# Two bursts of scatters moved on GpSimd's queue, and the second norm's application moved on ScalarE's, in a cross-attention and mixture-of-experts kernel

## The chip, the cores and the metric

The kernel runs on one core of a Trainium2 chip. The metric is the device time of one execution in microseconds (us), lower is better. The engines are named as in the profile: PE (TensorE, matmuls), PEld (its weight loads), DVE (VectorE), ACT (ScalarE), POOL (GpSimd) and SP (SyncE, which only issues DMAs here).

## What is computed

x has 4 x 2048 tokens of 512 values, the context 4 x 154. The reference is, cut to what matters:

```python
x = x + xattn(layernorm(x), ctx)          # 16 heads of 32, scores over 154 context rows, softmax, output projection with bias
x = x + ffn(layernorm(x))                 # 8 experts, 512 to 512, the best 2 of each token
# in ffn:
router_logits = einsum('bsd,ed->bse', x, W_router) + b_router
topk_w, topk_idx = top_k(softmax(router_logits), 2)
out = einsum('bseo,bse->bso', einsum('bsd,eod->bseo', x, W_experts) + b_experts, sparse_weights)
```

## The kernel before

**Two phases.** The first phase runs over 16 blocks of 512 tokens (each of 4 tiles of 128 tokens). For a block it computes the first norm, the attention, the sum x1 with the residual, the second norm and the router, and then writes every normalized token twice to a table in HBM (`dispatched`), sorted by expert, with a scatter: one indirect DMA on POOL's queue for each tile of 128 tokens and each of the two choices. The second phase takes 135 tiles of 128 rows of that table one after the other, multiplies each with its expert's weights and adds the result to the output in HBM, again with an indirect DMA on POOL.

**Slots.** The first phase is software-pipelined by hand. Each engine has a function `pe_slot`, `act_slot`, `dve_slot`, `pool_slot`, `sp_slot` that writes out one slot: the steps of several blocks in a fixed order. All engines work through their slots in order and wait for one another by semaphores alone. One slot takes about 50 us in the profile, and a loop repeats them; the first and last slots are written out. In what follows a slot is named by the block b whose scores and exponentials it computes. In that slot the blocks b+1 to b+3 are in their first norm and query projection, block b-1 is in its output projection, and block b-2 is applied its second norm and scattered.

**The steps that the change and the prediction touch**, on POOL in the order of before:
- `pool_PL` (line 1172): the low half of the probabilities P, 128x1024, of parts 0, 2, 3, 5, 7, 8 of a block (parts 1, 4, 6, 9 are DVE's, line 1091). PE's `pe_PV` waits for them.
- `pool_NC` (lines 597 to 615): a chain of eight tiny operations that turns the variances into scale and shift. With n = 0 it is the first norm's of block b+3, with n = 1 the second norm's of block b-1. It waits for `act_norm` (ACT line 582).
- `pool_BX(j)` (line 1248): adds the output bias to the residual of tile j of block b-1. DVE's `dve_Oe(j)` (line 987) waits for it: it adds the output projection, which PE has left in a PSUM bank, and so also frees that bank.
- `pool_RQ` (lines 1192, 1195): prepares the router's logits; DVE's `dve_RB` (line 1012) waits for it. `pool_RP` and `pool_RW` (lines 1206 to 1239): masks, weights and rows of the router for block b-2.
- `pool_SC` and `pool_SD` (line 1252): the two bursts, four scatters each, of block b-2. Both wait for the second norm's result, `act_NY` (ACT line 620).

On PE, `pe_MT` (line 756) turns the row maxima of block b+1 for ACT's `act_MTe` (line 933), and `pe_LB` (lines 851 to 854), right behind it, computes the second part of the router's logits in 36 small matmuls. `pe_LB` may only begin when `dve_Oe(3)` has emptied its bank; behind it stands the seventh query step, `pe_Q` (line 708), which waits for `act_MTe`. From slot 13 on the first norm's chain is no longer there, and in slot 15 PE has neither queries nor maxima left to compute.

In slot 14 DVE also computes a table that assigns tiles to experts (`table_sums`, `table_experts`, `table_rows`, lines 1126 to 1161): some 25 operations on 8 values, which lie between its other steps.

Of the kernel before, what the change touches and what calls it, by code (L numbers as in the profile page):

```python
# [19 lines left out]
NB = N // TB  # L20
# [90 lines left out]
def build(nc, x, ctxT, wqT, bq, wkT, bk, wvT, bv, woT, bo, weT, be, wrT, br, wo, boc, out):  # L111
# [15 lines left out]
    def hold(e):  # L127

        e.sem_inc(tick[id(e)], 1)
# [266 lines left out]
    def act_split(e, n):  # L396

        name, dst, scale = parts_of[n]
        e.wait_ge(L[name], 16)
        src = w_sb[name] if name in w_sb else wr32[:, :, :]  # L400
        e.activation(dst[:, 0, :, :], src, ACT.Copy, scale=scale).then_inc(p_hi, 1)
# [174 lines left out]
    def act_norm(e, n, b):  # L576
        e.wait_ge(nvar[n], b.at(NJ, NJ))
        if b.past(1):
            e.wait_ge(nco[n], b.at(NCO))
        e.activation(nrm[n][:, 1, :], aggr[n][:, :, 1], ACT.Ln, bias=epst[:, 0:1]).then_inc(nln[n], 1)  # L580
        e.wait_ge(nln[n], b.at(1, 1))
        e.activation(nrm[n][:, 2, :], nrm[n][:, 1, :], ACT.Exp, scale=-0.5).then_inc(nrs[n], 1)
# [35 lines left out]
    def act_apply(e, n, b, j, src, dst):  # L618
        e.wait_ge(nco[n], b.at(NCO, NCO))
        e.activation(dst[:, j, 0:D], src[:, j, :], ACT.Identity, scale=nrm[n][:, 5, j:j + 1],  # L620
                     bias=nrm[n][:, 6, j:j + 1]).then_inc(nap[n], 1)
# [6 lines left out]
    def act_NY(e, b, j):  # L628
        if j == 0:
            for k in range(TOPK):  # L630
                if b.past(2):
                    e.wait_ge(scat[b.par][k], b.half(64))
        act_apply(e, 1, b, j, xR[b.par], xn2[b.par])
# [223 lines left out]
    def act_XTh(e, b, i):  # L857
        e.wait_ge(t1p, b.at(4, i + 1))
        if i == 0 and b.past(1):
            e.wait_ge(qp, b.at(4))  # L860
            e.wait_ge(lap, b.at(1))
        e.activation(xnT[0][:, i, :], W[:, BANK[f"XT{i}"], :], ACT.Copy).then_inc(t1h, 1)

    def act_Qh(e, b, G):
        if b.first and G == 0:
            e.wait_ge(p_bk, 2)
        e.wait_ge(qp, b.at(4, G + 1))
        if G == 0 and b.past(1):
            e.wait_ge(restack[1 - b.par], (b + -1).half(192, 192))
        e.activation(qs[0][:, G, :], W[:, BANK[f"Q{3 * G}"], :], ACT.Identity, bias=bqs[:, G:G + 1]).then_inc(qhe, 1)  # L870
        if b.first and G == 3:
            act_split(e, 2)

            e.wait_ge(qle, 4)
            restack_heads(e, b, (2, 3))

    def act_ATh(e, b, i):
        e.wait_ge(atp, b.at(4, i + 1))
        if i == 0 and b.past(1):
            e.wait_ge(op_, b.at(4))  # L880
            e.wait_ge(lbp, b.at(1))
        e.activation(aT[0][:, i, :], W[:, BANK[f"AT{i}"], :], ACT.Copy).then_inc(ath, 1)
# [32 lines left out]
    def exps(n):  # L915

        h = BANK[f"ST{n}"] - 2
        return P32[PLP.index(n) % R32][:, :, :] if n in PLP else S[:, 2 * h:2 * h + 2, :]

    def act_PH(e, b, n):  # L920
        e.wait_ge(exd, b.at(10, n + 1))

        done = (2 * n - 9) // 5 if n >= 5 else (2 * n + 11) // 5 - 4
        if n > 4 or b.past(1):
            e.wait_ge(pvt, b.at(8, 2 * done + 2))
        r = 2 * (n % 5)
        e.activation(Pst[0][:, r:r + 2, :], exps(n), ACT.Copy).then_inc(phd, 1)  # L927
# [241 lines left out]
    def pool_PL(e, b, n):  # L1169
        e.wait_ge(phd, b.at(10, n + 1))  # L1170
        r = 2 * (n % 5)
        e.tensor_tensor(Pst[1][:, r:r + 2, :], exps(n), Pst[0][:, r:r + 2, :], ALU.subtract).then_inc(pldp, 1)  # L1172
# [77 lines left out]
    def scatter(e, p, k):  # L1250
        for j in range(NJ):
            e.indirect_dma_start(xs_d.ap(), bass.IndirectOffsetOnAxis(ap=idx[p][:, k * NJ + j:k * NJ + j + 1], axis=0),  # L1252
                                 xn2[p][:, j, :], None).then_inc(scat[p][k], 16)

    def pool_SC(e, b):
        e.wait_ge(ridx, b.at(1, 1))
        e.wait_ge(rwd, b.at(RWD, RWD))
        e.wait_ge(nap[1], b.at(NJ, NJ))
        hold(e)
        scatter(e, b.par, 0)  # L1260

    def pool_SD(e, b):
        e.wait_ge(ridx, b.at(1, 1))
        e.wait_ge(rwd, b.at(RWD, RWD))
        e.wait_ge(nap[1], b.at(NJ, NJ))
        hold(e)
        scatter(e, b.par, 1)
# [27 lines left out]
    def restack_heads(e, b, heads):  # L1295
        p = b.par
        for g in heads:
            for part, row in ((0, 0), (0, 32), (1, 64)):
                e.dma_start(Qst[p][row:row + 32, g::4, :], qs[part][32 * g:32 * g + 32, :, :]).then_inc(restack[p], 16)
# [170 lines left out]
    def act_slot(e, s):  # L1470
        bm2, bm1, b, bp1, bp2, bp3 = s + (-2), s + (-1), s, s + 1, s + 2, s + 3
        on_bm2, on_bm1, on_b, on_bp1, on_bp2, on_bp3 = bm2.here(), bm1.here(), b.here(), bp1.here(), bp2.here(), bp3.here()
        if on_b:
            act_EX(e, b, 1)
            act_PH(e, b, 0)
            act_PH(e, b, 1)
            act_EX(e, b, 2)
        if on_bp1:
            act_Qh(e, bp1, 3)
        if on_bm1:  # L1480
            act_ATh(e, bm1, 0)
        if on_b:
            act_PH(e, b, 2)
        if on_bm1:
            act_ATh(e, bm1, 1)
        if on_b:
            act_EX(e, b, 3)
            act_EX(e, b, 4)
        if on_bm1:
            act_ATh(e, bm1, 2)  # L1490
            act_ATh(e, bm1, 3)
        if on_b:
            act_PH(e, b, 3)
            act_PH(e, b, 4)
            act_EX(e, b, 5)
        if on_bp2:
            act_XTh(e, bp2, 0)
        if on_b:
            act_PH(e, b, 5)
            act_EX(e, b, 6)  # L1500
        if on_bm2 and not bm2.last:
            act_RX(e, bm2)
        if on_b:
            act_PH(e, b, 6)
            act_EX(e, b, 7)
        if on_bp2:
            act_XTh(e, bp2, 1)
            act_XTh(e, bp2, 2)
        if on_b:
            act_PH(e, b, 7)  # L1510
            act_EX(e, b, 8)
        if on_bp2:
            act_XTh(e, bp2, 3)
        if on_b:
            act_EX(e, b, 9)
            act_PH(e, b, 8)
            act_PH(e, b, 9)
        if on_bp3 and not bp3.first:
            act_norm(e, 0, bp3)
        if on_bp2:  # L1520
            act_Qh(e, bp2, 0)
        if on_bp3:
            act_NX(e, bp3, 0)
        if on_bp2:
            act_Qh(e, bp2, 1)
            act_WEh(e, bp2)
        if on_bm2 and not bm2.last:
            act_NY(e, bm2, 0)
            act_NY(e, bm2, 1)
            act_NY(e, bm2, 2)  # L1530
            act_NY(e, bm2, 3)
        if on_bp3:
            act_NX(e, bp3, 1)
        if on_bp1:
            act_MTe(e, bp1)
        if on_bm1 and not bm1.last:
            act_norm(e, 1, bm1)
        if on_bp3:
            act_NX(e, bp3, 2)
            act_NX(e, bp3, 3)  # L1540
        if on_bp2:
            act_Qh(e, bp2, 2)
        if on_bp1:
            act_EX(e, bp1, 0)
# [90 lines left out]
            dve_SN(e, bm2, 2)  # L1635

    def pool_slot(e, s):
        bm1, b, bp1, bp2, bp4 = s + (-1), s, s + 1, s + 2, s + 4
        on_bm1, on_b, on_bp1, on_bp2, on_bp4 = bm1.here(), b.here(), bp1.here(), bp2.here(), bp4.here()
        if on_bp1:  # L1640
            pool_PL(e, bp1, 2)
        if on_bm1 and not bm1.last:
            pool_RP(e, bm1)
        if on_bp1:
            pool_PL(e, bp1, 3)
        if on_b:
            pool_BX(e, b, 0)
        if on_bp1:
            pool_RC(e, bp1)
        if on_b:  # L1650
            pool_BX(e, b, 1)
            pool_BX(e, b, 2)
        if on_bm1 and not bm1.last:
            pool_RW(e, bm1)
        if on_bp1:
            pool_PL(e, bp1, 5)
        if on_bp4:
            pool_NC(e, bp4, 0)
        if on_bp1:
            pool_PL(e, bp1, 7)  # L1660
            pool_PL(e, bp1, 8)
        if on_b:
            pool_BX(e, b, 3)
        if on_bm1 and bm1.here(NB - 3):
            pool_SC(e, bm1)
        if on_b and not b.last:
            pool_NC(e, b, 1)
            pool_RQ(e, b)
        if on_bm1 and bm1.here(NB - 3):
            pool_SD(e, bm1)  # L1670
        if on_bp2:
            pool_PL(e, bp2, 0)

# [395 lines left out]
```

## Time and profile before

| | |
|---|---|
| median of 3 runs | 1279.43 us (1275.38 to 1282.6) |
| span of the profiled execution | 1340.9 us |
| PE busy | 1224.7 us, 91% |
| DVE busy | 881.3 us, 66% |
| POOL busy | 744.6 us, 56% |
| ACT busy | 722.1 us, 54% |
| mean granted TensorE clock | 0.950 |

The profiled execution has no other time of its own than its span, and that is 61.5 us above the median of the timed runs. Busy time counts an engine's instructions; waits are shown as idle time before the instruction that waited, with the name of what ended the wait. The first phase lasts until about 893 us of the profile, the second from there to the end.

### The profile page before, as it was taken

The numbers are of one execution on the slowest core, as the hardware profiler recorded it, in microseconds if no ns is written. First come the engines' busy times: TensorE is split into PE (matmuls) and PEld (weight loads), VectorE is DVE, ScalarE is ACT, GpSimd is POOL, SyncE is SP. The second block draws the span as 40 slices with busy tenths as digits, with TensorE's granted clock in tenths as the row PEclk, the third lists the DMA queues.
The fourth block names the chain that finished last, engine by engine and source line by source line (L and its number), as shares of the span: only waits on it lengthen the run. The fifth ranks groups of instructions, "written<-read, shape, count | busy, mean of one in ns | idle before, by whom it ended". The sixth has DMA issues, their size and how long they took to land. (4 is left out here: it accounts for less than half of the span.)

```text
span 1340.9 us, 36001 instructions
## 1 busy us (share of the span) xinstructions
PE 1224.7 (91%) x11024; PEld 735.1 (55%) x11025; DVE 881.3 (66%) x1933; ACT 722.1 (54%) x1040; POOL 744.6 (56%) x980
## 2 busy tenths in 40 slices
PE   8887999998999989999999986869899999999997
PEld 4445665655655655665655654534354555555454
DVE  4657787877868867867877867545445555555454
ACT  4336875775775775775766662624333333334333
POOL 4003555675675675675675674864644445444545
PEclk9879999999989998989989997889999999999999
DMA  8842664584583574583583573967999989998886
GB/s 267 253 135 65 173 176 153 148 254 142 150 258 130 142 241 152 147 262 131 144 237 115 132 215 109 357 221 156 199 177 184 175 173 188 179 172 155 168 165 133
DMA packets 135547, 239.22 MB, mean 178 GB/s; under 512 B 18440, under 2 KB 49416, under 8 KB 134280
## 3 DMA queue, kind: packets, MB, share of 16 engines
q1 hardware_dynamic: 102391, 161.24, 41.2%
q0 software_dynamic: 29808, 67.73, 25.2%
q10 hardware_dynamic: 3232, 8.68, 1.9%
q8 instruction: 78, 1.28, 0.4%
q14 instruction: 38, 0.30, 0.1%
HBM read 112.00 MB, written 101.40 MB: 159 GB/s over the span
## 5 line engine op out<-in xcount | busy, mean ns | idle before, releaser
L1854 PE MATMUL S<-we_s,wq_s 128*128 x1620 | 376.3, 382 | 12.6 <-DVE att L1832 5.8
L1782 POOL DMA_INDIRECT out<-xn,to x135 | 208.9, 1547 | 212.7 <-DMA out<-xn,to 123.6
L1854 PEld LDWEIGHTS S<-we_s,wq_s 128*128 128x128 f16 x1620 | 158.1, 98 | 180.8 <-issue 22.3
L1172 POOL TENSOR_TENSOR we_s<-P_s,we_s 128x1024 f16<-128x1024 f32 x96 | 204.2, 2136 | 65.6 <-ACT we_s L927 65.3
L1793 ACT ACTIVATE wq_s<-PVp 128x512 f16<-128x512 f32 x137 | 81.6, 597 | 272.4 <-PE PVp L1844 247.1
L1252 POOL DMA_INDIRECT dispatched<-xn,idx x128 | 131.7, 1029 | 92.6 <-ACT xn L620 52.1
L975 DVE TENSOR_REDUCE mx_sb<-S 128x6 f32<-128x924 f32 x160 | 171.3, 1111 | 11.3 <-PE S L726 9.1
L708 PE MATMUL W<-we_s,wq_s 128*128 128x512 f16 x512 | 168.7, 409 | 8.7 <-ACT mT L933 5.3
L746 PE MATMUL W<-wo_s,aT_hi 128*128 128x512 f16 x512 | 164.5, 383 | 2.6 <-DVE aT_lo L953 1.4
L1832 DVE SCALAR_TENSOR_TENSOR att<-S,be_s 128x512 f32<-128x512 f32 x135 | 93.3, 691 | 111.0 <-PE S L1854 101.5
L1810 DVE TENSOR_TENSOR wq_s<-PVp,wq_s 128x512 f16<-128x512 f32 x137 | 94.6, 691 | 38.3 <-ACT wq_s L1793 35.1
L818 PE MATMUL PVp<-Vm,we_s 128*128 128x33 f16 x3072 | 118.9, 179 | 0.0
L1091 DVE TENSOR_TENSOR we_s<-S,we_s 128x1024 f16<-128x1024 f32 x64 | 78.1, 1220 | 52.0 <-ACT we_s L927 51.9
L726 PE MATMUL S<-Kst,we_s 96*128 96x154 f16 x1024 | 99.2, 233 | 13.8 <-DVE we_s L1091 7.6
L870 ACT ACTIVATE we_s<-W,bqs 128x512 f16<-128x512 f32 x64 | 43.9, 688 | 123.9 <-PE W L708 123.9
L927 ACT ACTIVATE we_s<-P_s 128x1024 f16<-128x1024 f32 x96 | 101.4, 1057 | 11.8 <-PE PVp L818 9.3
L726 PEld LDWEIGHTS S<-Kst,we_s 96*128 96x128 f16 x1024 | 78.5, 99 | 52.5 <-DVE mx_sb L975 8.2
L818 PEld LDWEIGHTS PVp<-Vm,we_s 128*128 128x128 f16 x3072 | 106.9, 97 | 0.0
L708 PE MATMUL W<-xnT_lo,wq_s 128*128 128x512 f16 x256 | 104.8, 409 | 2.2 <-issue 2.2
L1800 ACT ACTIVATE xn<-att,wt 128x512 f32<-128x512 f32 x135 | 96.3, 714 | 12.1 <-DVE att L1832 5.2
L909 ACT ACTIVATE P_s<-S 128x1024 f32<-128x1024 f32 x96 | 98.1, 1022 | 6.7 <-issue 4.1
L746 PE MATMUL W<-wo_s,aT_lo 128*128 128x512 f16 x256 | 98.0, 383 | 0.0
(207 smaller groups left out, 2039.8 us busy)
## 6 DMA issues: line engine op xcount, KB each, us to landing
P_s<-dispatched SPq DMA_DIRECT2D x139, 260.5 KB
we_s<-we_s SPq DMA_DIRECT2D x186, 128.0 KB, 6.0
be_s<-in_x SPq DMA_DIRECT2D x16, 1024.0 KB, 9.1
xR_s<-in_x SPq DMA_DIRECT2D x16, 1024.0 KB
out<-xR_s SPq DMA_DIRECT2D x16, 1024.0 KB
wst<-in_weT SPq DMA_DIRECT2D x16, 512.0 KB, 6.2
we_scratch<-wsp SPq DMA_DIRECT2D x16, 512.0 KB, 5.5
Kst<-k_scratch SPq DMA_DIRECT2D x16, 480.0 KB, 5.1
```

The costliest lines, as they stand in the source:

```text
L708: m = e.matmul(W[:, bank, :], wq_s[:, wp, k, G * P:(G + 1) * P], xnT[xp][:, k, :], start=(n == 0), stop=(n == 11))
L726: m = e.matmul(S[:, 2 * (BANK[f"MX{n}"] - 2) + u % 6 // 3, (u % 3) * C:(u % 3 + 1) * C], Qst[p][0:96, h, j * P:(j + 1) * P], Kst[p][0:96, ...
L746: m = e.matmul(W[:, bank, :], aT[ap][:, k, j * P:(j + 1) * P], wo_s[:, wp, k, :], start=(n == 0), stop=(n == 11))
L818: m = e.matmul(o[:, g * 33:(g + 1) * 33], Pst[pp][:, (5 * G + g) % 10, tok], Vm[p][:, 4 * G + g, vv, :], start=False, stop=True, skip_grou ...
L909: e.activation(P32[i % R32][:, :, :], at, ACT.Exp, scale=1.0 / (SS * ROOT)).then_inc(exd, 1)
L927: e.activation(Pst[0][:, r:r + 2, :], exps(n), ACT.Copy).then_inc(phd, 1)
L975: e.tensor_reduce(mx_sb[:, 6 * n:6 * n + 6].rearrange("p (a k) -> p a k", a=2), S[:, 2 * h:2 * h + 2, 0:3 * C].rearrange("p a (k c) -> p a ...
L1172: e.tensor_tensor(Pst[1][:, r:r + 2, :], exps(n), Pst[0][:, r:r + 2, :], ALU.subtract).then_inc(pldp, 1)
L1252: e.indirect_dma_start(xs_d.ap(), bass.IndirectOffsetOnAxis(ap=idx[p][:, k * NJ + j:k * NJ + j + 1], axis=0), xn2[p][:, j, :], None).then_ ...
L1782: e.indirect_dma_start(out, bass.IndirectOffsetOnAxis(ap=to[u][:, :], axis=0), yw[u % YW], None, bounds_check=N - 1, oob_is_err=False, com ...
L1800: e.activation(yw[u % YW], yb[u % 2], ACT.Copy, scale=wt[u][:, 0:1]).then_inc(ywd, 1)
L1854: m = e.matmul(Yp[:, u % 2, :], gT[u % 2][xp][:, k, :], we_s[:, bass.ds(n * WN + (wp * KC + k) * D, D)], start=(c == 0), stop=(c == 11))
```

## The change

In the text of `act_slot` the four applications of the second norm move ahead: two stand before the first query step's evacuation (`act_Qh(0)`), two behind it and before the first norm's first application. In `pool_slot` the second burst, `pool_SD`, leaves the end of the slot and stands one slot later, behind part 5 of P and ahead of the first norm's chain; the first burst, `pool_SC`, changes places with `pool_BX(3)`. Nothing is added or taken away.

```diff
@@ act_slot
             act_norm(e, 0, bp3)
+        if on_bm2 and not bm2.last:
+            act_NY(e, bm2, 0)
+            act_NY(e, bm2, 1)
         if on_bp2:
             act_Qh(e, bp2, 0)
+        if on_bm2 and not bm2.last:
+            act_NY(e, bm2, 2)
+            act_NY(e, bm2, 3)
         if on_bp3:
             act_NX(e, bp3, 0)
         if on_bp2:
             act_Qh(e, bp2, 1)
             act_WEh(e, bp2)
-        if on_bm2 and not bm2.last:
-            act_NY(e, bm2, 0)
-            act_NY(e, bm2, 1)
-            act_NY(e, bm2, 2)
-            act_NY(e, bm2, 3)
         if on_bp3:
             act_NX(e, bp3, 1)
@@ pool_slot
         if on_bp1:
             pool_PL(e, bp1, 5)
+        if on_bm2 and bm2.here(NB - 3):
+            pool_SD(e, bm2)
         if on_bp4:
             pool_NC(e, bp4, 0)
         if on_bp1:
             pool_PL(e, bp1, 7)
             pool_PL(e, bp1, 8)
-        if on_b:
-            pool_BX(e, b, 3)
         if on_bm1 and bm1.here(NB - 3):
             pool_SC(e, bm1)
+        if on_b:
+            pool_BX(e, b, 3)
         if on_b and not b.last:
             pool_NC(e, b, 1)
             pool_RQ(e, b)
-        if on_bm1 and bm1.here(NB - 3):
-            pool_SD(e, bm1)
```

(POOL's own slot number runs one behind the slot's name as used in the text, so its `bm1` is block b-2 there.)

On POOL, one slot of the loop from part 5 of P (the first row) on; `xn` are the normalized tokens and `nrm` the norm's chain. Before:

```order
L1172 TENSOR_TENSOR we_s<-P_s,we_s 128x1024 x2
L1248 TENSOR_TENSOR xR_s<-xR_s,bo_b 128x512
L1252 DMA dispatched<-xn_0,idx 66688x521 x4
L597 TENSOR_SCALAR nrm<-aggr 128x4
```

Now:

```order
L1172 TENSOR_TENSOR we_s<-P_s,we_s 128x1024
L1265 REGISTER_ALU
L1252 DMA dispatched<-xn_1,idx 66688x521 x4
L588 REGISTER_ALU
L590 REGISTER_ALU
L595 REGISTER_ALU
L597 TENSOR_SCALAR nrm<-aggr 128x4
```

The four scatters of the second burst, of the block before (the other buffer), stand between part 5 of P and the first norm's chain; further down in the same slot (not shown) the first burst stands ahead of the bias addition instead of behind it.

Slot 15 has no chain of the first norm. On POOL, from the router's last row of that slot on, before:

```order
L1239 TENSOR_TENSOR xn2_1<-hot 128x4x8
L1172 TENSOR_TENSOR we_s<-P32_s,we_s 128x1024 x3
L1248 TENSOR_TENSOR xR_s<-xR_s,bo_b 128x512
L1252 DMA dispatched<-xn2_1,idx1 66688x521 x4
L597 TENSOR_SCALAR nrm1<-aggr1 128x4
```

Now:

```order
L1239 TENSOR_TENSOR xn2_1<-hot 128x4x8
L1172 TENSOR_TENSOR we_s<-P32_s,we_s 128x1024
L1252 DMA dispatched<-xn2_0,idx0 66688x521 x4
L1172 TENSOR_TENSOR we_s<-P32_s,we_s 128x1024 x2
L1252 DMA dispatched<-xn2_1,idx1 66688x521 x4
L1248 TENSOR_TENSOR xR_s<-xR_s,bo_b 128x512
L597 TENSOR_SCALAR nrm1<-aggr1 128x4
```

Ahead of the bias addition of block 14's last tile (line 1248) there were three parts of P; now there are three parts of P and eight scatters.

## Rows read from the trace of the kernel before

**Rows 1.** The profile page's head: span of the profiled execution.

```profile
span 1340.9 us, 36001 instructions
```

**Rows 2.** Waits of PE (engine, line, waited for: us in all, times, longest).

```profile
PE W L854 <- issue: 15.1, 21, 2.0
```

**Rows 3.** Timeline of POOL, slot 7 (start us, us, what [idle before <- releaser]).

```profile
450.31 2.13 POOL L1172 TENSOR_TENSOR we_s<-P_s,we_s 128x1024 f16<-128x1024 f32 x1
...
456.47 0.22 POOL L597 TENSOR_SCALAR nrm<-aggr 128x4 f32<-128x4 f32 x1 [4.02 <-ACT nrm L582]
...
462.97 1.26 POOL L1248 TENSOR_TENSOR xR_s<-xR_s,bo_b 128x512 f32<-128x512 f32 x1
...
467.98 1.08 POOL L1252 DMA_INDIRECT dispatched<-xn,idx  x1 [3.74 <-ACT xn L620]
...
471.89 0.96 POOL L1252 DMA_INDIRECT dispatched<-xn,idx  x1 [0.30 <-issue]
...
479.21 1.08 POOL L1252 DMA_INDIRECT dispatched<-xn,idx  x1 [0.62 <-issue]
```

**Rows 4.** Timeline of DVE, slot 7: last output tile; router's logits.

```profile
470.25 0.68 DVE L987 SCALAR_TENSOR_TENSOR xR_s<-W,xR_s 128x512 f32<-128x512 f32 x1
...
478.73 0.68 DVE L1012 SCALAR_TENSOR_TENSOR lg<-lgs,nrm,lgq 128x8 f32<-128x8 f32 x4 [3.04 <-POOL lgq L1195]
```

**Rows 5.** Timeline of PE: slot 7 around MT and LB, with scatters in flight.

```profile
470.99 0.60 PE L756 MATMUL W<-ident,mx_sb 128*16 128x128 f32 x4
...
471.43 0.25 PE L851 MATMUL W<-wx_s,aT_hi 128*128 128x16 f16 x4
...
474.69 0.61 PE L708 MATMUL W<-we_s,wq_s 128*128 128x512 f16 x2 [0.27 <-ACT mT L933]
```

**Rows 6.** Timeline of PE: slot 1, the same place, before any scatter.

```profile
175.31 0.60 PE L756 MATMUL W<-ident,mx_sb 128*16 128x128 f32 x4
...
175.75 0.25 PE L851 MATMUL W<-wx_s,aT_hi 128*128 128x16 f16 x4
...
176.68 0.61 PE L708 MATMUL W<-we_s,wq_s 128*128 128x512 f16 x2
```

**Rows 7.** PE's granted clock (PEclk) and busy times in two stretches.

```profile
425.30:428.50 3.20, 3.20 (x9) 1.06 (x8) 0.46 (x4) 0.75 (x2) 1.51 (x8) 0.50 0.85 299
...
706.00:779.00 73.00, 67.86 (x782) 43.82 (x781) 56.80 (x104) 43.31 (x62) 43.43 (x66) 1.00 0.44 134
```

**Rows 8.** Timelines of POOL and DVE, slot 8, the same places.

```profile
501.75 2.13 POOL L1172 TENSOR_TENSOR we_s<-P_s,we_s 128x1024 f16<-128x1024 f32 x1
...
520.79 0.68 DVE L987 SCALAR_TENSOR_TENSOR xR_s<-W,xR_s 128x512 f32<-128x512 f32 x1
```

**Rows 9.** Timeline of POOL, slot 15.

```profile
852.60 6.31 POOL L1172 TENSOR_TENSOR we_s<-P_s,we_s 128x1024 f16<-128x1024 f32 x3
...
858.88 1.25 POOL L1248 TENSOR_TENSOR xR_s<-xR_s,bo_b 128x512 f32<-128x512 f32 x1
...
865.25 0.23 POOL L597 TENSOR_SCALAR nrm<-aggr 128x4 f32<-128x4 f32 x1
...
868.27 0.25 POOL L1195 TENSOR_TENSOR lgq<-lgq,br_b 128x32 f32<-128x32 f32 x1 [0.18 <-POOL lgq L1192]
```

**Rows 10.** Timelines of DVE and PE, slots 15 and 16.

```profile
860.84 0.69 DVE L987 SCALAR_TENSOR_TENSOR xR_s<-W,xR_s 128x512 f32<-128x512 f32 x1 [2.85 <-PE W L746]
...
868.62 0.72 DVE L1012 SCALAR_TENSOR_TENSOR lg<-lgs,nrm,lgq 128x8 f32<-128x8 f32 x4 [1.42 <-issue]
...
878.86 0.61 PE L746 MATMUL W<-wo_s,aT_hi 128*128 128x512 f16 x1 [1.42 <-DVE aT_lo L953]
```

**Rows 11.** Timelines of DVE, POOL and PE, slot 14, around the table.

```profile
800.85 3.91 DVE L1126 TENSOR_TENSOR scan<-scan 128x8 f32<-128x8 f32 x2
...
800.52 6.29 POOL L1172 TENSOR_TENSOR we_s<-P_s,we_s 128x1024 f16<-128x1024 f32 x3
...
812.22 0.95 PE L726 MATMUL S<-Kst,we_s 96*128 96x154 f16 x6 [7.58 <-DVE we_s L1091]
```

More of the change, by code:

```diff
@@ L1637, in pool_slot @@
     def pool_slot(e, s):
-        bm1, b, bp1, bp2, bp4 = s + (-1), s, s + 1, s + 2, s + 4
-        on_bm1, on_b, on_bp1, on_bp2, on_bp4 = bm1.here(), b.here(), bp1.here(), bp2.here(), bp4.here()
+        bm2, bm1, b, bp1, bp2, bp4 = s + (-2), s + (-1), s, s + 1, s + 2, s + 4
+        on_bm2, on_bm1, on_b, on_bp1, on_bp2, on_bp4 = bm2.here(), bm1.here(), b.here(), bp1.here(), bp2.here(), bp4.here()
         if on_bp1:
@@ L1661, in pool_slot @@
             pool_PL(e, bp1, 8)
+        if on_bm1 and bm1.here(NB - 3):
+            pool_SC(e, bm1)
         if on_b:
             pool_BX(e, b, 3)
-        if on_bm1 and bm1.here(NB - 3):
-            pool_SC(e, bm1)
         if on_b and not b.last:
@@ L1668, in pool_slot @@
             pool_RQ(e, b)
-        if on_bm1 and bm1.here(NB - 3):
-            pool_SD(e, bm1)
         if on_bp2:
```

## The prediction

> **What bounds the kernel now.** I read the page first, then the waits by engine, then the timelines of single slots. The timed runs have a median of 1279.43 us, the profiled execution a span of 1340.9 us [rows 1]: it ran 61.5 us longer than what is to be predicted, so I first have to find what of the trace is in the timed runs at all. In a slot PE works almost without a pause, and POOL, whose order changes, waits: in slot 7 it stands idle 4.02 us before the first norm's chain and 3.74 us before the first burst [rows 3]. Nothing that POOL does in the middle slots is what PE waits for last.
>
> The one large idle place of PE is the step LB. In slot 1, before any scatter exists, it takes from 175.75 to 176.68, 0.9 us [rows 6]. In slot 7 it begins at 471.43 and the query step behind it at 474.69, 3.3 us, while the first burst runs on POOL from 467.98 to 472.85 [rows 3, 5]. From the row maxima's step (MT) to that query step it is 1.37 us in slot 1 and 3.70 us in slot 7, so 2.3 us are lost. The waits list them as "issue": 15.1 us at line 854 alone [rows 2]. Just after such an LB the granted clock is at 0.50 for some 3.4 us, that is 1.2 GHz, after PE had stood still in between; over 73 us from 706 on it stays at 2.4 GHz [rows 7]. Twelve such LBs at 2.3 us are 28 us. With low-clock stretches that cost about 1.6 us each (half of 3.2 [rows 7]), one or two in a slot, it comes to 45 to 60 us, which is just the 61.5 us by which the profile is longer. Nothing else in the trace is of that size. So I take it that LB's gaps and most of what follows from them belong to the profiled execution, and are not there in the timed runs. This is an inference from two totals, and the first rival is that it is wrong.
>
> **The change part by part.**
>
> *Second norm applied sooner (ACT).* No instruction is added. The first two stand where ACT waits for PE, the other two where it waits for POOL's norm chain; POOL reaches the first burst later than that anyway (below). Cost and gain: 0. If that cover were gone, the first query step's evacuation would be late by what they take. Nobody waits for it within that time, since DVE has two maxima to reduce first.
>
> *Second burst a slot later (POOL).* Four scatters take 471.89 + 0.96 - 467.98 = 4.87 us, and 0.62 us pass before the first [rows 3]: 5.5 us. They leave the place behind the router's preparation, where only POOL itself gains. They come behind part 5 of P, whose end is 450.31 + 2.13 = 452.44, so they end at 457.9. The first norm's chain started at 456.47, after a wait; it starts 1.5 us later. The chain and parts 7 and 8 take 462.97 - 456.47 = 6.5 us [rows 3] and end at 464.4.
>
> *First burst ahead of the bias addition (POOL).* Its 5.5 us bring POOL to 469.9, and the last bias addition, 1.26 us, ends at 471.2 instead of 464.2 [rows 3]. Behind it waits DVE's last output tile, which began at 470.25 [rows 4]. So a wait of 0.9 us appears that was not there. From the end of part 5 the whole chain is 0.62 + 4.87 + 6.5 + 0.62 + 4.87 + 1.26 = 18.7 us. In slot 8 the same interval is only 520.79 - 503.88 = 16.9 us [rows 8], and the wait 1.8 us. DVE's tile takes 0.68 us and frees the bank for LB: in slot 7 it was done at 470.93, LB began at 471.43 [rows 4, 5], so 0.5 us, less about 0.1 for the signal, are slack. PE waits 0.5 us in slot 7 and 1.4 us in slot 8. Slots 3 to 12 have all the parts, ten of them. I take 0.8 us for each, between the two: **+8 us**, with bounds of +4 and +14. Behind LB, in a slot without gaps, stands a query step that waits for nothing else [rows 6], so this goes straight into the slot. DVE's two norm statistics behind the tile are late as well, and the router's logits after them, for which DVE waits 3.04 us now [rows 4]; I let that cost nothing. Slot 13 has no first chain, and 2.3 us more room.
>
> *Slot 15.* Here POOL goes through P without a wait: parts 5, 7 and 8 take 852.60 to 858.9, and the bias addition is done at 860.1 [rows 9], just ahead of DVE's tile at 860.84 [rows 10]. Now both bursts stand before it: 854.7 + 5.5 + 4.2 + 5.5 + 1.25 = 871.2. DVE's tile, and LB behind it, are late by 10.3 us, and PE has nothing else in its queue there. Statistics and variances (about 1.8 us), ACT's norm (0.6) and the chain with the router's preparation (868.52 - 865.25 = 3.3 [rows 9]) put DVE's router logits at 871.8 + 5.7 = 877.5 instead of 868.62 [rows 10], 8.9 us. From these to the output projection of block 15 are now 10.2 us (878.86 [rows 10]). DVE needs about half of that for the work itself; the rest are waits beside scatters in flight, which are then over. So that step starts between 4.4 and 8.9 us later. I take **+7 us**. Behind it PE goes on to the second phase, where I know of no wait long enough to take this back.
>
> *Slot 14, the table.* Two additions on 8 values take 3.91 us on DVE while POOL works on three parts of P in a row, 6.29 us, and PE stands still for 7.58 us after it [rows 11]. Now the second burst stands between the first and the second of these parts. If DVE's small operations pass beside scatters, DVE comes to its next step about 3.7 us sooner. But four more such additions stand a little further on, and by my sum they then meet parts 7 and 8. So I take **0**, with bounds of -3.5 and 0. The Trainium skill (SBUF — State Buffer, "Who interferes with whom") says that a DVE instruction with two SBUF inputs fully blocks against a GpSimd one that reads SBUF, and infers that descriptor generation needs the write side alone. The 3.91 us agree with the first half; no row here shows the second. By it the first additions would pass, and the sum would be 3.5 us less if the later ones passed too.
>
> *LB beside the first burst.* The burst moves from 468.0-472.9 to about 465.0-469.9, and LB to 471.9. The gaps should go from the trace: -28 us of the span and perhaps -10 for the clock. In the timed runs I take 0 of it; the bounds are 0 and -38.
>
> **Sum.** 1279.43 + 8 + 7 + 0 + 0 = 1294.4 us for the timed runs. For the span: 1340.9 + 15 - 28 - 10 = about 1318 us, so I expect the profile to become shorter while the timed runs become longer.
>
> **The rivals.**
> 1. *LB's gaps are in the timed runs too, at least in part* (chance 0.18). For it: each of them stands beside scatters, none where there are none [rows 5, 6]; against it: the 61.5 us that are then unexplained. The slots win 12 x 2.3 = 28 us and some 12 us of clock, less the 15 us above: 1279.4 - 25 = 1254 us. It decides once more than half of the 28 us is real. A third of it gives 1281.
> 2. *The waits are swallowed* (0.15). The timed runs' POOL may be ahead of the profiled one by the 0.9 to 1.8 us that the bias addition is late, and slot 15 costs its lower bound: +4.4 us and little else, 1284 us or less. For it speaks that busy spans on POOL are rough, and that POOL's work before part 5 follows DVE and PE closely. Against it: in slot 15 the 10.3 us are far too much to vanish.
> 3. *The new waits lower the clock* (0.06). PE would stand still for about 0.8 us among small matmuls in ten slots, and a stretch at 1.2 GHz costs 1.6 us [rows 7]: up to +16 on top, 1310 us. Against it: with all waits of PE that it has now, the stretch from 706 to 779 stays at 2.4 GHz.
>
> **How the numbers follow.** My forecast has 0.61, with a range of its own from 1286 (4 + 4.4 us, less some of the table) to 1303 (14 + 8.9). 0.5% of the time, 6.4 us, is about what a measurement of this kernel can tell from no change. Slower by more than that, over 1285.8: 0.61 + 0.06 = 0.67. Within it: 0.15. Faster, under 1273: rival 1 with 0.18. The range that holds 8 in 10 leaves out rival 3 and most of rival 1, but takes in its weaker forms: 1268 to 1304.
>
> **What would show it.** In the timeline of DVE the last output tile of slots 3 to 12 waits 0.9 to 1.8 us for POOL's line 1248, and in slot 15 for about 10 us; LB begins late by 0.5 to 1.4 and by about 10 us. The "issue" waits at lines 851 and 854 shrink to a small part, and stretches at 1.2 GHz get fewer. POOL's wait before the first chain is gone. The prediction is wrong if the tile does not wait, if PE makes up the 10 us of slot 15 before the second phase, or if the timed runs fall along with the span.

## The result, and the profile after

The changed kernel takes 1288.4 us (median of 12 runs) where the kernel before takes 1281.64 in as many: a ratio of 1.005 with a 95% interval of 1.0033 to 1.0067, slower by 6.8 us. The forecast was 1294.4. The profiled execution of the changed kernel has a span of 1286.5 us and a time of its own of 1288.22. It belongs to the timed ones, which the profile of before, with its 1340.9 us [rows 1], did not.

The page of the changed kernel: span, busy times, granted clock in 40 slices.

```profile
span 1286.5 us, 36005 instructions
...
PE 1194.3 (93%) x11024; PEld 718.5 (56%) x11025; DVE 879.7 (68%) x1933; ACT 722.3 (56%) x1040; POOL 749.8 (58%) x980
...
PEclk9979999999999999999999978898999999999999
```

The timeline of the changed kernel in slot 8, which answers to [rows 3 to 6] and [rows 8]: start, duration, engine, operation, and in brackets the idle time ahead of it and what ended it.

```profile
475.65 2.13 POOL L1172 TENSOR_TENSOR we_s<-P_s,we_s 128x1024 f16<-128x1024 f32 x1
477.94 1.10 POOL L1252 DMA_INDIRECT dispatched<-xn,idx  x1 [0.16 <-issue]
...
485.24 4.22 POOL L1172 TENSOR_TENSOR we_s<-P_s,we_s 128x1024 f16<-128x1024 f32 x2
...
489.61 1.08 POOL L1252 DMA_INDIRECT dispatched<-xn,idx  x1 [0.15 <-issue]
...
494.52 1.28 POOL L1248 TENSOR_TENSOR xR_s<-xR_s,bo_b 128x512 f32<-128x512 f32 x1
...
495.44 0.60 PE L756 MATMUL W<-ident,mx_sb 128*16 128x128 f32 x4
...
495.91 0.69 DVE L987 SCALAR_TENSOR_TENSOR xR_s<-W,xR_s 128x512 f32<-128x512 f32 x1 [1.12 <-POOL xR_s L1248]
...
496.75 0.24 PE L851 MATMUL W<-wx_s,aT_hi 128*128 128x16 f16 x4 [0.71 <-DVE xR_s L987]
...
497.65 0.59 PE L708 MATMUL W<-we_s,wq_s 128*128 128x512 f16 x2
```

POOL goes from part 5 of P to the bias addition without a wait: 18.0 us from 477.78 to 495.80 (18.7 in the working). DVE's output tile waits 1.12 us for it, LB begins late, and the query step comes 2.21 us after MT instead of 1.37. Over slots 3 to 12 that excess is 0 to 0.91 us, 5.1 us together. It is not all: behind that query step PE waits once more, 3.7 us in nine of the ten slots, for DVE's router logits (line 1012), which are late for the same reason; the lines stand below. The gaps of LB are gone, and the granted clock is 1.00, that is 2.4 GHz, in the whole stretch of slots 3 to 12.

The same in slot 15, which answers to [rows 9, 10].

```profile
803.26 2.13 POOL L1172 TENSOR_TENSOR we_s<-P_s,we_s 128x1024 f16<-128x1024 f32 x1
...
805.54 1.10 POOL L1252 DMA_INDIRECT dispatched<-xn,idx  x1 [0.16 <-issue]
...
810.46 4.21 POOL L1172 TENSOR_TENSOR we_s<-P_s,we_s 128x1024 f16<-128x1024 f32 x2
...
812.64 0.51 PE L815 MATMUL PVp<-Vr,we_s 128*128 128x132 f16 x3 [4.67 <-POOL we_s L1172]
...
819.64 1.27 POOL L1248 TENSOR_TENSOR xR_s<-xR_s,bo_b 128x512 f32<-128x512 f32 x1
...
821.02 0.69 DVE L987 SCALAR_TENSOR_TENSOR xR_s<-W,xR_s 128x512 f32<-128x512 f32 x1 [12.31 <-POOL xR_s L1248]
...
821.86 0.24 PE L851 MATMUL W<-wx_s,aT_hi 128*128 128x16 f16 x4 [2.53 <-DVE xR_s L987]
```

The output tile waits 12.31 us. But PE had already waited 4.67 us, for part 7 of P, which the second burst now delays. That wait was in no step of the prediction.

### The profile page after: what moved, and what is told of

It is laid out like the page before. It is cut to its first block and busy times, and to the rows that moved or that the text cites. A ratio compares the mean times of both kernels' runs of the same rounds, so it can differ in the third digit from the quotient of the medians.

```text
span 1286.5 us, 36005 instructions
## 1 busy us (share of the span) xinstructions
PE 1194.3 (93%) x11024; PEld 718.5 (56%) x11025; DVE 879.7 (68%) x1933; ACT 722.3 (56%) x1040; POOL 749.8 (58%) x980
## 5 line engine op out<-in xcount | busy, mean ns | idle before, releaser
L1172 POOL TENSOR_TENSOR we_s<-P_s,we_s 128x1024 f16<-128x1024 f32 x96 | 211.8, 2214 | 101.9 <-ACT we_s L927 101.8
L708 PE MATMUL W<-we_s,wq_s 128*128 128x512 f16 x512 | 158.9, 388 | 8.8 <-DVE lg L1012 3.9
L1252 POOL DMA_INDIRECT dispatched<-xn,idx x128 | 126.5, 988 | 35.2 <-issue 32.8
L708 PE MATMUL W<-xnT_lo,wq_s 128*128 128x512 f16 x256 | 99.1, 387 | 2.3 <-issue 2.3
L815 PE MATMUL PVp<-Vr,we_s 128*128 128x132 f16 x768 | 86.5, 221 | 7.8 <-POOL we_s L1172 5.4
```

The costliest lines, as they stand in the source:

```text
L708: m = e.matmul(W[:, bank, :], wq_s[:, wp, k, G * P:(G + 1) * P], xnT[xp][:, k, :], start=(n == 0), stop=(n == 11))
```

## The experiments

The diffs are against the changed kernel unless said otherwise. Ratios are to the kernel before on the same device, with 95% intervals.

### First group: four kernels on a device where everything is slower

On this device the kernel before took 1324.6 us (median of 35 runs) instead of 1281.6. In the two later groups, on two other devices, it took 1281.35 and 1282.29.

**e1_before_again**: the kernel before, no edit.

> The kernel before, unchanged, profiled once more. If the gaps in LB and the drops of the clock belong to that one profiled execution, as I inferred, this profile has a span near its timed runs (about 1280 us), MT to the query step behind it takes 1.4 us instead of 3.7 in slots 2 to 13, and the clock is at 2.4 GHz from about 120 to 750 us. If they are a property of the kernel whenever it is profiled, the span is again about 1340 us with clock 0.95. If they are in the timed runs too, the cores' spans listed with the timed runs are bimodal or the gaps are there in a profile whose span is near 1280. Ratio to before: 1.000, which also shows how far two measurements of one program differ.

1321.93 us, 0.9976 [0.9953, 0.9998]: two measurements of one program differ by 0.2%. The timeline of slot 7 of this execution, whose time of 1314.02 us is that of a timed run:

```profile
461.04 0.60 PE L756 MATMUL W<-ident,mx_sb 128*16 128x128 f32 x4
...
461.94 0.96 POOL L1252 DMA_INDIRECT dispatched<-xn,idx  x1 [0.30 <-issue]
...
464.61 0.60 PE L708 MATMUL W<-we_s,wq_s 128*128 128x512 f16 x2 [0.27 <-ACT mT L933]
```

The gaps of the first profile [rows 5] are there, 3.51 to 3.64 us from MT to the query step in slots 2 to 13, in an execution that was timed. So they are not made by profiling: the profile of b1_before_look below, on another device, has none. They come with the device, or with the session on it, since each of these devices was used once.

**e2_bias_first**: the bias addition ahead of the first burst again.

```diff
+        if on_b:
+            pool_BX(e, b, 3)
         if on_bm1 and bm1.here(NB - 3):
             pool_SC(e, bm1)
-        if on_b:
-            pool_BX(e, b, 3)
```

> The changed kernel with the last bias addition ahead of the first burst again in every slot; the second burst and the second norm stay moved. My theory (the bias addition is late and holds up DVE's last output tile, then LB): the waits of DVE at L987 for line 1248 in slots 3 to 12 (0.55 to 1.19 us) are gone, which gives back the 5 us of LB's delay, and in slot 15 the bias addition comes some 5 us sooner, which gives 3 to 5 us: 8 to 10 us faster than the changed kernel, 1279 us, 0.997 to 1.000 of before. Rival (the loss comes from the second burst's place ahead of the first norm's chain and from the second norm's order on ScalarE): no better than the changed kernel, 1.004 to 1.006 of before.

1320.04 us, 0.997 [0.9947, 0.9994]. The ratio is in the range that was expected, but on a device with stalls that bears nothing out, and the changed kernel did not run beside it. In slots 3 to 12 the last output tile waits for no bias addition and LB has no gaps, yet these slots take 481.86 us, hardly less than the 485.80 of e1_before_again, where PE stands still in every LB. The waits and the timeline of slot 11 in this kernel show where PE stands still instead:

```profile
PE S L726 <- issue: 22.2, 14, 3.6
```

```profile
652.95 0.56 PE L726 MATMUL S<-Kst,we_s 96*128 96x154 f16 x6
...
654.69 0.96 POOL L1252 DMA_INDIRECT dispatched<-xn,idx  x1 [0.30 <-issue]
655.00 1.12 DVE L975 TENSOR_REDUCE mx_sb<-S 128x6 f32<-128x924 f32 x1 [2.16 <-PE S L726]
...
656.18 0.44 PE L726 MATMUL S<-Kst,we_s 96*128 96x154 f16 x4 [1.80 <-issue]
```

The scores for the maxima were computed at 652.95, but DVE took them up at 655.00, and PE went on at 656.18. On this device the stall goes with the burst to whatever lies beside its last scatters. This order, with the bias addition right ahead of the first burst in every slot, was not run on a device without stalls.

**e3_norm_only**: the kernel before with ScalarE's edit alone (the first hunk of the change).

> The kernel before with the edit on ScalarE alone. POOL's order is that of before, so no bias addition is late. The first burst no longer waits 3.74 us for the second norm and so starts sooner than the row maxima's step. My theory (this edit costs and gains nothing, LB's gaps are not in the timed runs): 0.998 to 1.002 of before. Rival A (LB's gaps, or part of them, are in the timed runs): the burst is over before LB begins, and the kernel is faster than before, by up to 28 us, 0.98 to 0.995. Rival B (the order on ScalarE is what costs 6.8 us in the changed kernel): 1.003 to 1.007.

1332.63 us, 1.0077 [1.0044, 1.0109]. LB's gaps are mostly gone (the issue waits at line 854 are 4.8 us in all, against 13.2 in e1_before_again), and PE waits 25.3 us at line 726 for DVE's maxima, against 5.2; the ten slots take 493.7 us, 7.9 more. Rival A falls even here: a burst that starts sooner moves the stall, it doesn't remove it. Rival B (1.003 to 1.007) has its number here, but with a cause that the other devices do not show. What this edit does alone on a device without stalls was not run; e10_first_only below has it together with the first burst's move and takes 1.0007, so it does not cost 6.8 us there unless that move gives them back.

**e4_slot15**: in slot 15 the bias addition ahead of both bursts.

```diff
+        if b.reg is None and b.c == NB - 2:
+            pool_BX(e, b, 3)
         if on_bm2 and bm2.here(NB - 3):
             pool_SD(e, bm2)
...
-        if on_b:
+        if on_b and not (b.reg is None and b.c == NB - 2):
             pool_BX(e, b, 3)
```

> The changed kernel with one difference in slot 15 alone: the last bias addition stands ahead of both bursts and of parts 5, 7, 8's rest. DVE's last output tile there waits 12.31 us for it in the changed kernel; here it should not wait for it. PE's wait of 4.67 us for part 7 of P, which the second burst delays, stays. If slot 15's 7 us were rightly sized and due to the bias addition: 5 to 7 us faster than the changed kernel, 1282 to 1283 us, 1.000 to 1.002 of before. Rival (what PE waits for in slot 15 is the delayed part 7, and the output tile's delay is given back before the second phase): within 2 us of the changed kernel, 1.004 to 1.006 of before.

1320.91 us, 0.998 [0.9959, 1.0]. The changed kernel did not run on this device, and the stalls are larger than what is asked, so the question was put again below.

### Second group: a device without stalls

**a1_after_again**: the changed kernel, no edit. **b1_before_look**: the kernel before, a single execution.

> The changed kernel, unchanged, together with the three below. It shows how it stands to before on the device on which these four run: on the device of the first comparison before took 1281.6 us and the changed kernel 1.005 of it; on the device of the four experiments before it, before took 1324.6 us and its profile had LB's gaps. My theory: where before takes about 1282 us there are no gaps and the ratio is again 1.003 to 1.007; where before takes about 1324 us, stalls beside the scatters are there in both kernels, only at other places, and the ratio is 0.998 to 1.004. Rival: on a device with stalls the changed kernel is rid of them, since its bursts are over when LB begins, and the ratio is below 0.99.

> The kernel before, for its profile on the same device. My theory: if this device times it at about 1282 us, MT to the query step behind it takes 1.4 us in slots 2 to 13, no issue wait stands at LB, and DVE's last output tile does not wait for the bias addition; the slots are then 45 to 46 us long. If it times it at about 1324 us, the gaps are there as in the first profile (3.5 to 3.8 us). Rival: the gaps are there at 1282 us too, and the difference between devices is elsewhere (the second phase, the clock).

a1_after_again took 1285.82 us, 1.0044 [1.0023, 1.0065], as in the first comparison. b1_before_look took 1279.55 us, with no gap: from MT to the query step 1.37 to 1.45 us in all slots from 1 to 13. This is the profile of before that the prediction would have needed. Four stretches of it: from MT of slot 3 to MT of slot 13, to MT of slot 14, to the first expert matmul, to the end (start and end, length, busy time and count of PE, its weight loads, DVE, ACT and POOL, granted clock, DMA share, GB/s).

```profile
265.43:728.66 463.23, 446.01 (x5447) 290.85 (x5443) 389.97 (x803) 339.95 (x466) 324.78 (x493) 1.00 0.63 191
728.66:780.12 51.46, 41.78 (x511) 26.30 (x507) 42.74 (x92) 26.63 (x34) 32.24 (x44) 0.90 0.53 161
780.12:843.08 62.96, 51.19 (x566) 32.17 (x563) 32.79 (x96) 32.14 (x45) 48.08 (x78) 0.81 0.84 311
843.08:1277.90 434.82, 414.81 (x2205) 222.20 (x2203) 222.19 (x592) 167.21 (x277) 226.58 (x171) 0.99 0.88 177
```

The same stretches of the changed kernel (a1_after_again):

```profile
263.84:722.87 459.03, 444.07 (x5446) 289.78 (x5443) 391.22 (x804) 339.23 (x466) 328.51 (x492) 1.00 0.63 192
722.87:775.31 52.44, 40.33 (x511) 26.61 (x507) 43.67 (x92) 26.44 (x34) 30.66 (x42) 0.90 0.47 142
775.31:843.64 68.33, 50.40 (x568) 31.87 (x563) 32.55 (x96) 32.13 (x45) 44.32 (x73) 0.85 0.76 277
843.64:1278.40 434.76, 413.84 (x2205) 221.68 (x2203) 221.96 (x592) 167.63 (x277) 230.33 (x177) 1.00 0.88 178
```

The ten slots are 4.2 us *shorter* after the change, although LB is late in nine of them. The reason is in slot 8 of b1_before_look:

```profile
497.78 0.60 PE L756 MATMUL W<-ident,mx_sb 128*16 128x128 f32 x4
...
499.23 0.61 PE L708 MATMUL W<-we_s,wq_s 128*128 128x512 f16 x2
...
504.23 1.08 POOL L1252 DMA_INDIRECT dispatched<-xn,idx  x1 [0.62 <-issue]
...
509.56 4.22 POOL L1172 TENSOR_TENSOR we_s<-P_s,we_s 128x1024 f16<-128x1024 f32 x2
...
513.84 0.35 PE L815 MATMUL PVp<-Vr,we_s 128*128 128x132 f16 x3 [0.99 <-POOL we_s L1172]
```

The second burst begins at 504.23, parts 0 and 2 of P come behind it in one piece at 509.56, and PE waits 0.99 us for part 2. Such a wait of 0.51 to 1.03 us stands in eight of the ten slots, 6.5 us together. A second wait that this kernel has and the changed one has not is for the DMA that brings the row maxima to the scores (line 786): 3.1 us in five of the ten slots. After the change, in slot 8 of a1_after_again, it is POOL that waits, for ACT:

```profile
502.89 2.98 POOL L1172 TENSOR_TENSOR we_s<-P_s,we_s 128x1024 f16<-128x1024 f32 x1 [1.52 <-ACT we_s L927]
...
507.51 2.13 POOL L1172 TENSOR_TENSOR we_s<-P_s,we_s 128x1024 f16<-128x1024 f32 x1 [1.64 <-ACT we_s L927]
```

The delay of the last output tile goes on to the router. In b1_before_look and in a1_after_again, slot 8:

```profile
503.75 0.68 DVE L1012 SCALAR_TENSOR_TENSOR lg<-lgs,nrm,lgq 128x8 f32<-128x8 f32 x4 [1.43 <-POOL lgq L1195]
504.49 0.60 PE L708 MATMUL W<-we_s,wq_s 128*128 128x512 f16 x2
```

```profile
501.50 0.64 DVE L1012 SCALAR_TENSOR_TENSOR lg<-lgs,nrm,lgq 128x8 f32<-128x8 f32 x4 [1.42 <-POOL lgq L1195]
502.20 0.61 PE L708 MATMUL W<-we_s,wq_s 128*128 128x512 f16 x2 [0.45 <-DVE lg L1012]
```

DVE's router logits begin 5.97 us after MT (497.78) before the change and 7.19 us after it (494.31) now, 1.22 us later, and PE's next query step, which did not wait before, waits 0.45 us for them. In a1_after_again that wait stands in nine of the ten slots, 3.8 us together, beside the 5.4 us by which the step behind LB is late.

Of the waits of PE (us in all, times, longest), in b1_before_look, in a1_after_again, and in e10_first_only, which keeps the second burst at its old place (below):

```profile
PE PVp L815 <- POOL we_s L1172: 8.6, 11, 1.0
```

```profile
PE PVp L815 <- POOL we_s L1172: 5.4, 2, 4.7
...
PE W L851 <- DVE xR_s L987: 6.9, 9, 2.7
```

```profile
PE PVp L815 <- POOL we_s L1172: 12.0, 12, 1.8
```

**e4b_slot15**: the kernel e4_slot15 once more. **e5_bias_early**: the bias addition of the last tile right behind those of tiles 1 and 2, in every slot.

```diff
             pool_BX(e, b, 2)
+            pool_BX(e, b, 3)
...
-        if on_b:
-            pool_BX(e, b, 3)
```

> The same kernel as e4_slot15, once more, now beside the changed kernel on one device: in slot 15 alone the last bias addition stands ahead of both bursts. Its difference to the changed kernel is what the late bias addition costs in slot 15. My sum had +7 us for the slot; PE's wait of 4.67 us for part 7 of P stays in this kernel, so 3 to 5 us faster than the changed kernel is what remains if the size was right; under 2 us if the second phase gives the delay back.

> The changed kernel with the last bias addition right behind those of tiles 1 and 2, in every slot. No output tile of DVE can then wait for it. Theory (the late bias addition is the loss): the 5 us of the ten slots and the 3 to 5 us of slot 15 come back: 8 to 10 us faster than the changed kernel and 0.997 to 1.000 of before on a device without stalls. Rival (part 5 of P, which now comes 1.26 us later, the router's rows and what waits for them take its place): no more than 3 us faster than the changed kernel.

e4b_slot15: 1285.4 us, 1.0034 [1.0012, 1.0055], against 1.0044 of the changed kernel, so the rival holds: in slot 15 the late bias addition costs next to nothing while PE waits for part 7, 5.54 us in this kernel. e5_bias_early: 1277.52 us, 0.9976 [0.996, 0.9993], 8.3 us faster than the changed kernel, as expected; its ten slots take 453.41 us, 5.6 less. PE's waits at LB and for the router's logits, 8.0 us in the ten slots of a1_after_again, are gone; some of what they cost comes back in smaller waits elsewhere.

### Third group: another device without stalls

**e6_second_only**: the kernel before with `pool_SD` moved alone. **e10_first_only**: the changed kernel with `pool_SD` back at the slot's end.

```diff
             pool_PL(e, bp1, 5)
-        if on_bm2 and bm2.here(NB - 3):
-            pool_SD(e, bm2)
...
             pool_RQ(e, b)
+        if on_bm1 and bm1.here(NB - 3):
+            pool_SD(e, bm1)
```

(e10_first_only; for e6_second_only the same lines with the signs turned, in the kernel before.)

> The kernel before with the second burst alone moved; the first burst stays behind the bias addition and ScalarE's order is that of before. New theory: in the profile of before on the device that times it at 1279.6 us PE waits 0.5 to 1.0 us in ten slots for a low part of P that POOL reaches late, because the second burst stands ahead of it; that was hidden where LB's gaps made room. So slots 3 to 13 get 8 to 10 us shorter, slots 14 and 15 together some 5 us longer: 0.995 to 0.999 of before on a device without LB's gaps. Rival, my prediction's reading (the second burst's old place costs nobody but POOL): the slots gain nothing and slot 15 costs: 1.002 to 1.005.

> The changed kernel without the second burst's move: the first burst is ahead of the bias addition and the second norm is applied sooner on ScalarE, the second burst stays at the slot's end. New theory: the bias addition ends near 469.7 of the old trace, so DVE's output tile waits hardly (0 to 0.3 us), PE's waits for P stay as they are in before, and in slot 15 the bias addition is 5.5 us late but part 7 of P is not: 1.000 to 1.004 of before. Rival (the first burst ahead of the bias addition is what costs the 5 us at LB, whatever stands ahead of it): 1.004 to 1.009.

**e8_ends_undone**: e5_bias_early with the second bursts of blocks 12 and 13 at their old places. **e9_slots_only**: the changed kernel with these two bursts, and the bias addition of slots 14 and 15, at their old places. The lines of the second bursts, the same in both (those of e9_slots_only for the bias addition are not shown):

```diff
-        if on_bm2 and bm2.here(NB - 3):
+        if on_bm2 and bm2.here(NB - 3) and not (b.reg is None and b.c >= NB - 2):
             pool_SD(e, bm2)
...
             pool_RQ(e, b)
+        if b.reg is None and b.c >= NB - 3 and bm1.here(NB - 3):
+            pool_SD(e, bm1)
```

> e5_bias_early with the second bursts of blocks 12 and 13 back in their old places, so that slots 14 and 15 have the order of before but for the early bias addition. If slot 15 costs what its traces say (the first expert tile 5.4 us later after slot 14's row maxima in the changed kernel, 5.6 in e5_bias_early) and slot 14 another 1 to 4: some 7 us faster than e5_bias_early, that is 0.990 to 0.994 of before on a device without LB's gaps, and faster than both kernels. Rival (the second phase or the other waits of the tail take it back): 0.996 to 1.000, as e5_bias_early.

> The changed kernel in all slots up to 13, with the POOL order of before in slots 14 and 15. It splits the result: if the ten slots gain 4 us net (waits of 5 us at LB against 9 us of waits for P that went away) and the last two slots cost 7 to 9, this kernel takes 0.995 to 0.999 of before. Rival, my prediction's sum (slots +8, slot 15 +7): 1.003 to 1.007.

Times, ratios and the stretches of each profile, in us, beside those above:

| kernel | time | ratio | slots 3 to 12 | slot 14 stretch | slot 15 stretch | second phase |
|---|---|---|---|---|---|---|
| b1_before_look | 1279.55 | | 463.2 | 51.5 | 63.0 | 434.8 |
| a1_after_again | 1285.82 | 1.0044 | 459.0 | 52.4 | 68.3 | 434.8 |
| e4b_slot15 | 1285.4 | 1.0034 | 458.7 | 53.8 | 68.0 | 436.8 |
| e5_bias_early | 1277.52 | 0.9976 | 453.4 | 55.5 | 68.6 | 438.1 |
| e6_second_only | 1283.7 | 1.0004 [0.9983, 1.0025] | 455.9 | 53.4 | 67.0 | 440.9 |
| e10_first_only | 1283.8 | 1.0007 [0.9979, 1.0035] | 460.8 | 53.6 | 64.2 | 439.6 |
| e9_slots_only | 1279.43 | 0.9966 [0.9944, 0.9987] | 458.9 | 55.5 | 61.8 | 439.7 |
| e8_ends_undone | 1270.26 | 0.9913 [0.9885, 0.9941] | 452.8 | 55.1 | 63.2 | 433.2 |

What follows. With the second burst alone moved the ten slots gain 7.3 us. With the first burst and ScalarE's edit they gain 2.4, with all of it 4.2, and with all of it and an early bias addition 9.8 to 10.4, about 7.3 + 2.4. So the second burst's old place cost some 7 us, the late bias addition costs 5.6 net, and LB's wait needs both bursts ahead of the bias addition: in the ten slots of e6_second_only and e10_first_only DVE's last output tile doesn't wait for it. The 2.4 us come although PE waits more for POOL in e10_first_only than before (8.6 us against 6.5 in the ten slots). What goes away is the wait for the row maxima's DMA: 3.1 us in b1_before_look and in e6_second_only, 0.2 in e10_first_only and e5_bias_early, none in a1_after_again. It goes with ScalarE's edit or with the first burst's move; no run has one without the other on a device without stalls. The slot 15 stretch is 67.0 to 68.6 us in all four kernels that have the second burst ahead of part 7, and 61.8 to 64.2 where it is not. e6_second_only was expected at 0.995 to 0.999: its slots gained a little less than the 8 to 10 us expected, and its end lost 6.0 instead of 5. e10_first_only, e9_slots_only and e8_ends_undone came as expected, and e8_ends_undone is faster than both kernels, by 0.9% than before.

## Why the prediction was right, and where it was not

**LB's gaps belong to the profiled execution only, 0 of them in the timed runs.** Right for the sum: b1_before_look has none at 1279.55 us. Wrong in the reason given. On the device of the first group the same gaps are in timed executions. The profile of before may have come from such a device, which was not shown: its 1340.9 us lie above all 35 timed runs of before there (highest 1334.32). The working's total was loose too: its row has 3.20 us at 1.2 GHz, not 3.4, and 28 us with one or two such stretches in each of twelve slots is 47 to 66 us, not 45 to 60. In e1_before_again the gaps make the ten slots 22.6 us longer than in b1_before_look, at a granted clock of 0.98.

**The waits for the bias addition in slots 3 to 12, +8 us, bounds 4 and 14.** The mechanism is as described: POOL's chain of 18.0 us, the output tile late by 0.27 to 1.19 us in the two traces of the changed kernel (one of ten slots had no wait in the first), LB late behind it. The size was 5.1 us in the first trace and 5.4 in a1_after_again, from the excess of MT to the query step over 1.37 us. **"The router's logits after them ...; I let that cost nothing"** failed: PE waits another 3.7 and 3.8 us for them in nine slots of the two traces. Part of both is given back within the slot. The net cost is what e5_bias_early takes away, 5.6 us. Rival 3 fell: with these waits the granted clock stays at 1.00 in the ten slots.

**"They leave the place behind the router's preparation, where only POOL itself gains."** This step failed. The second burst at the end of the slot stood ahead of parts 0 and 2 of P, and PE waited 0.51 to 1.03 us for part 2 in eight of the ten slots. In the trace that the prediction read, LB's gap of 2.3 us came just ahead of it and gave POOL the time, so the wait was not there to be seen (nor is it in e1_before_again, which has the same gaps). e6_second_only measures it, -7.3 us over ten slots. With the +5.6 of the term above and the -2.4 of e10_first_only, where the sum had 0 for ScalarE's edit, the slots came out 4.2 us shorter instead of 8 longer.

**Slot 15, +7 us, bounds 4.4 and 8.9.** The size is about right: the stretch is 5.4 us longer in a1_after_again. The carrier was another. Without the late bias addition (e4b_slot15, e5_bias_early) the stretch stays as long; without the second burst ahead of part 7 it is short again (e10_first_only, 64.2, where the bias addition still stands behind the first burst). PE's 4.67 us wait for part 7 was overlooked, since only DVE's queue was followed and not PE's.

**Slot 14, 0.** The table's operations did what the sum said. From b1_before_look, then from a1_after_again:

```profile
753.87 6.31 POOL L1172 TENSOR_TENSOR we_s<-P_s,we_s 128x1024 f16<-128x1024 f32 x3
...
758.13 2.07 DVE L1128 TENSOR_TENSOR tb<-scan 128x8 f32<-128x8 f32 x1
...
765.33 0.95 PE L726 MATMUL S<-Kst,we_s 96*128 96x154 f16 x6 [5.45 <-DVE we_s L1091]
```

```profile
749.55 1.10 POOL L1252 DMA_INDIRECT dispatched<-xn,idx  x1 [0.15 <-issue]
749.65 0.17 DVE L1128 TENSOR_TENSOR tb<-scan 128x8 f32<-128x8 f32 x1
...
753.92 4.78 DVE L1145 TENSOR_TENSOR took<-tb,scan 128x8 f32<-128x8 f32 x1
...
754.47 4.20 POOL L1172 TENSOR_TENSOR we_s<-P_s,we_s 128x1024 f16<-128x1024 f32 x2
...
760.16 0.95 PE L726 MATMUL S<-Kst,we_s 96*128 96x154 f16 x6 [8.33 <-DVE we_s L1091]
```

The same addition on two inputs of 8 values (line 1128) takes 2.07 us beside parts of P and 0.17 beside a scatter; a later one (line 1145), beside parts 7 and 8, takes 4.78. So the first ones pass and a later one meets the two parts. The 0.17 us agree with what the Trainium skill infers (SBUF — State Buffer, "Who interferes with whom"), that descriptor generation does not take what these operations need. The size was a little off: PE goes on at line 726 36.7 us after slot 13's MT in b1_before_look, 37.3 in a1_after_again, and 38.3 in the first profile of the changed kernel and in e4b_slot15, which have the same order there. The stretch is 51.5 us against 52.4, 53.7 and 53.8: +1.0 to +2.3 us, above the bounds of -3.5 and 0, with one execution of before to compare.

**The sum.** -4.2 + 5.4 + 1.0 in single executions is +2.2, and the timed runs have +5.6 (by the ratio 1.0044) and +6.8. The profiled execution of a1_after_again, 1280.17 us, is the shortest of its nine, so this sum is low. e9_slots_only puts -0.34% (4.4 us) on the slots, as its trace does; the rest, 8 to 10 us by the ratios (0.9976 against 0.9913, 1.0044 against 0.9966), is the order in slots 14 and 15, of which the traces of the same pairs show 5.7 and 3.5 before the first expert matmul. Where the other 2.4 to 6.5 us lie, stays open: the second phase varies from 433.2 to 440.9 us between single executions, and one execution of each doesn't resolve it. So "slower" came out as predicted in part by luck: the ten slots, forecast as half of the loss, gained, and the loss is in the order of slots 14 and 15, where another wait than the one named carries it. The change was forecast as +15 us and measured as +6.8.

## What to carry to other kernels

Compare the profile's time with the timed runs first; where they differ by several per cent, a gap in it may be absent there, and it may also hide a wait that is real, because it gives another engine time. When a step leaves its place, ask who is served by what stood behind it, as carefully as at its new place. In a pipeline that is written out, look at the first and last slots by themselves: the move of the second burst gained 7.3 us in the ten middle slots and lost about as much at the end (e6_second_only, 1.0004), and leaving it out there, with an early bias addition, made a kernel 0.9% faster than before.

## What the runs showed of the hardware

One device ran the same program 3.3% slower (1324.6 us against 1281.35 and 1282.29) with a granted clock that was little lower (median 0.959 over the runs of before, against 0.975 and 0.974). There PE, and what waits for it, stood still for 1.8 to 2.3 us beside the last scatters of the first burst, wherever this burst was put; in the profiles of the other devices no scatter was seen to stop it. An addition on two inputs of 128x8 on DVE took 0.17 us beside a scatter of POOL, and 2.07 and 4.78 us beside one and two of its 128x1024 operations of 2.1 us (slot 14 above). Neither the cause nor what marks such a device was found, and as each device was used once, device and session can't be told apart.
